# Graph attention on Trainium2: the clip of the exponentials moved from ScalarE and VectorE to GpSimd, the stage written without loops

## The reference

```python
q = (embeds[rows] @ qW).reshape(e, HEADS, dh)
k = (embeds[cols] @ kW).reshape(e, HEADS, dh)
v = (embeds[cols] @ vW).reshape(e, HEADS, dh)
scores = jnp.clip(jnp.einsum('ehd,ehd->eh', q, k), -10.0, 10.0)
exp_s = jnp.exp(scores)
norms = jax.ops.segment_sum(exp_s, rows, num_segments=nvar)[rows]
w = exp_s / (norms + 1e-08)
res = jax.ops.segment_sum(w[:, :, None] * v, rows, num_segments=nvar).reshape(nvar, d)
```

## Time and profile before

| | |
|---|---|
| median of 3 runs | 2467.38 us (2464.18 to 2469.9) |
| span of the profiled execution (its own time is given as this span) | 2467.5 us |
| VectorE busy in it | 1956.1 us |
| ScalarE busy in it | 1285.4 us |
| TensorE matmuls busy in it | 2131.4 us |
| GpSimd busy in it | 591.3 us |
| attention: first `masked` starts, last `sums_out` ends | 1007.83 us, 1489.84 us |

### The profile page before, as it was taken

One profiled execution on the slowest core, in us unless ns is written; L12 is line 12 of the kernel. 1 busy time (PEld: TensorE's weight loads), 2 busy tenths in 40 slices (PEclk: granted clock), 3 DMA queues, 4 the chain that ended last, 5 costly groups with the idle time before them and its releaser, 6 DMA issues. The chain is left out here.

```text
span 2467.5 us, 64202 instructions
## 1 busy us (share of the span) xinstructions
PE 2131.4 (86%) x22305; PEld 1792.1 (73%) x22306; DVE 1956.1 (79%) x2888; ACT 1285.4 (52%) x2996; POOL 591.3 (24%) x879
## 2 busy tenths in 40 slices
PE   2888887899999998776766666999999999999897
PEld 2777777899999998211111113799998599999787
DVE  8899998655565665899999996888887698888446
ACT  1888888333333332899999994432221622221323
POOL 3444443000000000200000001355554255555000
PEclk8999999899999999999999996999999999999799
DMA  2344444100010100511111113423233423232810
GB/s 67 147 165 170 167 168 160 69 29 28 28 41 29 41 15 14 140 47 41 42 42 41 42 41 129 138 73 85 73 86 64 181 72 86 72 86 45 299 43 21
DMA packets 94267, 205.36 MB, mean 83 GB/s; under 512 B 21204, under 2 KB 60756, under 8 KB 93952
## 3 DMA queue, kind: packets, MB, share of 16 engines
q1 hardware_dynamic: 80384, 182.39, 21.2%
q0 software_dynamic: 13696, 20.25, 4.3%
HBM read 116.99 MB, written 84.76 MB: 82 GB/s over the span
## 5 line engine op out<-in xcount | busy, mean ns | idle before, releaser
L1884 PE MATMUL l_bank<-tab,mask 128*128 128x192 f16 x7600 | 637.9, 247 | 7.3 <-PEq L1715 3.5
L1884 PEld LDWEIGHTS l_bank<-tab,mask 128*128 128x128 f16 x7600 | 630.9, 98 | 10.0 <-issue 9.3
L1470 DVE TENSOR_SCALAR mask<-code 128x1600 int32<-128x1600 int32 x304 | 543.7, 1815 | 95.8 <-PE l_bank L1884 70.6
L1860 POOL DMA_INDIRECT ggot<-table_dram,gidx x408 | 387.1, 949 | 265.4 <-PE l_bank L1884 204.9
L1351 DVE SCALAR_TENSOR_TENSOR pr<-ex,cring 128x1568 f32<-128x1568 f32 x200 | 356.3, 1782 | 0.0
L1289 PE MATMUL att_acc<-pr,v 128*32 128x392 f32 x1600 | 179.0, 520 | 147.6 <-DVE pr L1351 137.9
L891 PE MATMUL sums<-onehots,ct 128*128 128x192 f16 x3125 | 264.7, 248 | 11.3 <-issue 4.9
L891 PEld LDWEIGHTS sums<-onehots,ct 128*128 128x128 f16 x3125 | 261.8, 99 | 14.1 <-issue 7.6
L891 PE MATMUL sums<-u,ct 128*128 128x192 f16 x3125 | 259.1, 246 | 0.0
L891 PEld LDWEIGHTS sums<-u,ct 128*128 128x128 f16 x3125 | 258.0, 98 | 0.0
L1325 ACT ACTIVATE ex<-score_rest,poss 128x1176 f32<-128x1176 f32 x200 | 248.2, 1241 | 0.9 <-PE score_rest L1281 0.9
(11 more groups left out here) (349 smaller groups left out, 3143.0 us busy)
## 6 DMA issues: line engine op xcount, KB each, us to landing
code<-code_dram SPq DMA_DIRECT2D x38, 800.0 KB
code_dram<-flat SPq DMA_DIRECT2D x100, 200.0 KB, 1.9
ct_dram<-ct SPq DMA_DIRECT2D x25, 800.0 KB, 3.5
c_dram<-flat SPq DMA_DIRECT2D x25, 800.0 KB, 3.4
ct_again<-ct_dram SPq DMA_DIRECT2D x25, 800.0 KB, 16.9
cring<-c_dram SPq DMA_DIRECT2D x200, 98.0 KB, 1.9
table_dram<-tab SPq DMA_DIRECT2D x50, 384.0 KB, 2.3
flat<-code_dram SPq DMA_DIRECT2D x19, 800.0 KB, 4.4
```

Source lines behind the costliest of these rows:

```text
L1470: e.tensor_scalar(turned.rearrange("p (s q d) -> p s q d", q=NQ, d=DQ // 2), words.rearrange("p (q s d) -> p s q d", q=NQ, d=DQ // 2), abs ...
L1860: e.indirect_dma_start(ggot[:, k, j, :], None, table_dram[:, :], bass.IndirectOffsetOnAxis(ap=gidx[:, k, j:j + 1], axis=0)).then_inc(s_ggo ...
L1884: mm = e.matmul(acc[k][:, 0:2 * D], mask[:, r % MR, s, :], tab[:, s, r, :], start=(r == 0 and s == 0), stop=(r == R - 1 and s == NT - 1))
```

## The change

GpSimd clips the exponentials of all four heads on both sides with one `tensor_scalar` (min, max) of 128x1568 fp32, in place in `ex`, for each of the 200 tiles. VectorE is left with one `tensor_tensor` multiply of 128x1568 by the counts, which it reads from `cring` in SBUF as before. ScalarE has two plain Exps of 128x784, a pair of heads each, from two PSUM pairs. `acc` has two halves, so that the next block's sums start without waiting for the copy. AHEAD is 4. All eight blocks are written out without hardware loops. The relation weights are issued by SP at tile 27 and no longer by GpSimd; the maxima over them are taken at tile 75, and the `partition_all_reduce` stands behind GpSimd's last clip.

```diff
@@ gpsimd
+                        def clipped(n):
+                            e.wait_ge(s_ex[1], n + 1)
+                            ins = e.tensor_scalar(ex[n % UR][:], ex[n % UR][:], EXP_HIGH, EXP_LOW, ALU.min, ALU.max)
+                            ins.then_inc(s_clip, 1)
...
-                        load_relations(e, 0, s_bd_in)
+                        for n in range(TILES):
+                            clipped(n)
+                            if n == NT:
+                                e.wait_ge(s_pieces[2], 64)
+                                e.memset(bd[:], 0.0).then_inc(s_pad, 1)
+                                e.wait_ge(s_pad, 2)
                         e.wait_ge(s_bd, 2)
                         e.partition_all_reduce(btop[:], bmost[:], P, bass.bass_isa.ReduceOp.max).then_inc(s_bd, 1)
@@ sync
+                        for n in range(CR, TILES):
+                            if n in COPIES:
+                                load_copies(e, *COPIES[n])
+                            if n == RELATIONS_AT:
+                                e.wait_ge(s_pad, 2)
+                                load_relations(e, 0, s_bd_in)
+                            e.wait_ge(s_pr, n - CR + 1)
+                            load_counts(e, n)
@@ tensor
+                        for n in range(1, TILES):
+                            if n + AHEAD < TILES:
+                                scores(n + AHEAD, 0)
+                            sums(n)
+                            if n + AHEAD < TILES:
+                                scores(n + AHEAD, 1)
@@ scalar
-                            e.activation(short[j % UR][:], first_ps[:, 0:QC], ACT.Relu, bias=ten[:],
-                                         scale=negs[:]).then_inc(s_short, 1)
...
-                            e.activation(ex[j % UR][:, 1:H, :], rest_ps[j % 2][:, :, 0:QC], ACT.Exp,
-                                         scale=poss[:]).then_inc(s_rest, 1)
...
-                            e.activation(ex[j % UR][:, 0, :], short[j % UR][:], ACT.Exp, bias=ten[:],
-                                         scale=-1.0).then_inc(s_ex, 1)
...
+                        for n in range(TILES):
+                            for k in range(2):
+                                e.wait_ge(s_sc[k], n + 1)
+                                if k == 0 and n >= UR:
+                                    e.wait_ge(s_pr, n - UR + 1)
+                                e.activation(ex[n % UR][:, k * HP2:(k + 1) * HP2, :], pair_ps[k][:, :, 0:QC], ACT.Exp,
+                                             scale=poss[:]).then_inc(s_ex[k], 1)
@@ vector
-                            e.tensor_scalar(ex[j % UR][:, 1:H, :], ex[j % UR][:, 1:H, :], EXP_HIGH, None,
-                                            ALU.min).then_inc(s_capped, 1)
...
-                            e.scalar_tensor_tensor(pr[j % UR][:], ex[j % UR][:], EXP_LOW,
-                                                   cring[:, j % CR, :].unsqueeze(1).to_broadcast([P, H, QC]),
-                                                   ALU.max, ALU.mult).then_inc(s_pr, 1)
...
+                            e.wait_ge(s_c[n % CR], 16 * (n // CR + 1))
+                            e.wait_ge(s_clip, n + 1)
+                            if n >= UR:
+                                e.wait_ge(s_pv, n - UR + 1)
+                            e.tensor_tensor(pr[n % UR][:], ex[n % UR][:],
+                                            cring[:, n % CR, :].unsqueeze(1).to_broadcast([P, H, QC]),
+                                            ALU.mult).then_inc(s_pr, 1)
```

More of the change, by code:

```diff
@@ L1174, in _ @@
                         e.dma_start(vw[:], a["vW"]).then_inc(s_vw, 16)
-                        for j in range(CR):
-                            load_counts(e, 0, j)
+                        for n in range(CR):
+                            load_counts(e, n)
                         store_piece(e, 0)
@@ L1230, in gnn_kernel @@
                 UR = 5
-                short = [sb(f"short{k}", [P, QC], F32) for k in range(UR)]
                 ex = [sb(f"ex{k}", [P, H, QC], F32) for k in range(UR)]
                 pr = [sb(f"pr{k}", [P, H, QC], F32) for k in range(UR)]
-                ten = sb("ten", [P, 1], F32)
                 poss = sb("poss", [P, 1], F32)
[L1236 to L1241, removed]
+                HP2 = H // 2
+                pair_ps = [main.enter_context(nc.psum_tensor(f"score_pair{k}", [P, HP2, 512], F32)) for k in range(2)]
+                acc = main.enter_context(nc.psum_tensor("att_acc", [P, 2, 512], F32))
+                s_sc = [sem(f"l1_score{k}") for k in range(2)]
+                s_ex = [sem(f"l1_ex{k}") for k in range(2)]
+                s_cc, s_clip, s_pr, s_pv, s_acc, s_poss, s_pad = (
+                    sem("l1_" + k) for k in ("cc", "clip", "pr", "pv", "acc", "poss", "pad"))
                 s_bd, s_bd_in = sem("l1_bd"), sem("l1_bd_in")
-                AHEAD = 3
+                AHEAD, CAHEAD, OUT = 4, 3, 3
+                TILES = NQB * NT
+                RELATIONS_AT = NT + 2
+                LARGEST_AT = 3 * NT
                 with nc.Block() as block:
@@ L1270, in _, with scores @@
                     @block.tensor
                     def _(e):
-                        def scores(b, j, first=False):
-                            if first and j in first_keys:
+                        def scores(n, k):
+                            b, j = divmod(n, NT)
+                            if k == 0 and b == 0 and j in first_keys:
                                 e.wait_ge(s_spread[1][first_keys.index(j)], SPREAD)
[L1275 to L1287, removed]
+                            if k == 0 and n == NT:
+                                for piece in (1, 2):
+                                    e.wait_ge(s_spread[0][piece], SPREAD)
+                            if n:
+                                e.wait_ge(s_ex[k], n)
+                            for h in range(HP2):
+                                mm = e.matmul(pair_ps[k][:, h, 0:QC], ka[0:D, k * HP2 + h, j * P:(j + 1) * P],
+                                              qa[0:D, k * HP2 + h, b * QC:(b + 1) * QC], start=True, stop=True)
@@ L1288, in sums @@
+                            mm.then_inc(s_sc[k], 1)
+                        def sums(n):
+                            b, j = divmod(n, NT)
+                            e.wait_ge(s_pr, n + 1)
+                            if j == 0 and b >= 2:
+                                e.wait_ge(s_acc, b - 1)
                             for h in range(H):
-                                mm = e.matmul(acc[h * HW:(h + 1) * HW, 0:QC], v[:, j, h, :], pr[j % UR][:, h, :],
+                                mm = e.matmul(acc[h * HW:(h + 1) * HW, b % 2, 0:QC], v[:, j, h, :], pr[n % UR][:, h, :],
@@ L1293, in _ @@
                         first_keys = [b0 * QB // P for b0, _ in PIECES]
[L1294 to L1304, removed]
@@ L1306, in _ @@
-                        e.wait_ge(s_spread[0][0], SPREAD)
[L1307 to L1315, removed]
+                        FIRST = first_keys[1]
@@ new lines, in _ @@
+                        assert QC <= QB and 2 <= FIRST <= AHEAD
+                        e.wait_ge(s_spread[0][0], SPREAD)
+                        for n in range(FIRST):
+                            scores(n, 0)
+                            scores(n, 1)
+                        sums(0)
+                        for n in range(FIRST, AHEAD + 1):
+                            scores(n, 0)
+                            scores(n, 1)
+                        for n in range(1, TILES):
[4 more added lines that the diff above has]
+                                scores(n + AHEAD, 1)
@@ L1331, in _ @@
[L1331 to L1336, removed]
+                        e.wait_ge(s_poss, 1)
+                        for n in range(TILES):
[5 more added lines that the diff above has]
+                                             scale=poss[:]).then_inc(s_ex[k], 1)
@@ L1355, in sums_out @@
-                        def sums_out(b):
[L1357 to L1362, removed]
-                                    capped(b, j + 1)
-                                elif not last:
-                                    capped(b + 1, 0)
-                                masked(b, j)
-                                if first and j == NT - 1:
-                                    e.wait_ge(s_bd_in, 16 * LOADS)
-                                    e.tensor_reduce(bmost[0:D, 0:1], bd[0:D, :, 0:HW2], mybir.AxisListType.XY, ALU.max,
-                                                    apply_absolute_value=True).then_inc(s_bd, 1)
-                                    e.tensor_copy(bmost[:, 1:2], irregular[:]).then_inc(s_bd, 1)
-                                if j == 0 and not first:
-                                    sums_out(b - 1)
@@ L1385, in _, with masked @@
[L1385 removed]
+                        def masked(n):
+                            e.wait_ge(s_c[n % CR], 16 * (n // CR + 1))
```

(14 more changed lines are left out.)

31 lines of the change are left out of this document (3 added, 28 removed).

## The result

The changed kernel takes 2590.52 us (median of 4 runs, 2584.92 to 2592.64) against 2465.8 us before: 1.0501 times the time before, 95% interval 1.0485 to 1.0517, so 125 us slower. The forecast was 211 us slower, 2679 us. The sign and the mechanism were right, the size was not: the change costs 0.59 of what was forecast, and the time lies at the very lower edge of the range, 2590. (That bound was rounded down: 2612.5 less 0.1 us for each of 200 tiles is 2592.5, above what was measured.)

A forecast was written before the change was run, and what follows sets the result against it. VectorE was taken to bound attention at 2.38 us a tile; 1.70 multiply plus 1.72 clip made 3.42, +208 us over 200 tiles, plus 3 for weight loads, on 2467.5: 2679 us, range 2590 to 2930.

The forecast's parts named there:

- VectorE sets the kernel before; 2.38 us a tile: Attention before the change: VectorE, busy 419.44 of 419.50 us, sets the pitch at 2.38 to 2.39 us for 200 tiles.
- The multiply costs what `masked` did: VectorE's remaining multiply in attention was priced as `masked`: 1.78 us long and 1.70 us in pitch.
- Clip and multiply take turns, whoever came first: In attention, GpSimd's clip and VectorE's two-input multiply exclude each other, so their times add: pitch 3.42 us, +208 us.
- T = 1.72 us: GpSimd's two-sided clip of 128x1568 fp32 per attention tile, scaled from the 882 ns CAST of 806 elements: 1.72 us.
- The lower end of my bounds: GpSimd's clip in attention priced from below by a write-only iota, 0.89 ns an element: 1.39 us, pitch 3.09, total 2612.
- The page overruled: For GpSimd's clip, the skill page's 1.03 cycles per element, 1.35 us and a sum about 74 us lower, was set aside.
- The rival without turns: In attention, clip and multiply run side by side, ScalarE sets 1.86 us a tile: 2366 us, chance 0.10.
- The rival of a dear clip: In attention, turns with a clip of 2.0 to 3.0 us: 2734 to 2934 us, chance 0.24; above 3.0, 0.09.
- TensorE's clock may fall and costs nothing: In attention, TensorE at 1.2 instead of 2.4 GHz would need some 3.3 us a tile, under the pitch: costed at nothing.
- SP's 18 loads, one stall of 2 to 4 us: Weight loads issued ahead of tile 27's counts: 7.1 us of issue, 1.9 until counts land, +3 us in the sum.
- The reduction behind the last clip costs nothing: At attention's end, GpSimd's reduction takes 0.4 to 2.8 us beside VectorE's last multiply, the last sums and copy: nothing added.

The follow-up runs named there:

- half clip: The changed kernel with GpSimd clipping two of the four heads (128x784), the other two left unclipped: 2462.61 us (one run), 2.33 us a tile.

## Why the prediction was right and wrong

- **VectorE sets the kernel before; 2.38 us a tile**: right, 2.40 with the work at block ends (478.0 us for 199 pitches). The clip put on VectorE again gives 2.60, as its rows foretold.
- **The multiply costs what `masked` did**: right, 1787 ns where nothing disturbs it, against 1782.
- **Clip and multiply take turns, whoever came first**: right, in both directions, and no slower hand-over than their streams. What the trace before showed with operations of 6 and 25 elements holds for ones of 1568.
- **T = 1.72 us**: this step failed. The clip's term in the pitch is 1.30 us, 0.42 less, and 0.42 x 200 = 84 us is nearly the whole miss of 88 (2679 - 2590.5). With 1.30 the sum reads 2467.5 + 200 x 0.62 + 3 = 2594.5; the last 4 us are the tile before, which cost 2.40 us and not 2.38. Two errors lie in T. First the row, 0.23 us: I scaled the CAST's 882 ns by the elements, its fixed part with them; the clip, free, reads 1493 ns. Second, and nearly as large at 0.19: I took a free span for what one turn costs. GpSimd's own pitch would not have told it either, as the two free clips at the start of attention start 1.47 us apart. The half clip tells it: its shortest span is 829 ns against 1484 for the whole one, so 655 ns for 784 elements, 1.31 us of stream in a whole clip and some 0.17 fixed, and the 1.31 are what a turn was seen to cost. The lower end of my bounds, the iota's 0.89 ns an element, was the nearest: 1.39.
- **The page overruled.** I set aside the Trainium skill's figure (GPSIMD Engine Reference, Elementwise — side-by-side cycle accounting), 1.03 cycles per element or an estimated 1.35 us, because of the int32 TENSOR_SCALAR. The clip of fp32 read 1493 ns free and 1.30 us in the turns, so the estimate is near what a turn costs and 0.14 us short of the free span; by it the sum would have been 2605, 14 us over the measured time. The int32 row was the wrong witness; that its conversions make its price wasn't tried.
- **The rival without turns** (2366 us) is what the kernel does once the counts come from PSUM: 2364.7. That these agree to 2 us is luck: the rival had ScalarE at 1.86 us a tile, and the pitch is 1.77, with the start and the end of the stage longer. The rival of a dear clip (T over 2.0) is excluded.
- **TensorE's clock may fall and costs nothing**: it fell, to 0.83, and `sums` and `scores` still waited, for `pr` and for ScalarE.
- **SP's 18 loads, one stall of 2 to 4 us**: the trace of the changed kernel shows 7.2 us of issue and one wait of 2.5 us. The issue rows, then the row of waits:

```profile
1084.00 6.49 SPq L349 DMA_DIRECT2D spare<-in_weights  x16
...
1091.24 7.33 SPq L1131 DMA_DIRECT2D cring<-c_dram  x7
```

```profile
DVE pr L1345 <- DMA cring<-c_dram: 2.5, 1, 2.5
```

- **The reduction behind the last clip costs nothing**: nearly. It started 5.99 us behind GpSimd's last clip, with nothing that it waited for in the records, and so ended 0.8 us behind VectorE's last copy. A gap of 7.12 us of the same kind stands ahead of the first clip. The row of the reduction:

```profile
1611.51 0.37 POOL L1265 PARTITION_ALL_REDUCE btop<-bmost  x1 [5.99 <-issue]
```

  The Trainium skill (GPSIMD Engine Reference, Instruction dispatch) has about 6 us for a first call of freshly loaded code; the gap of 5.99 us agrees, the one of 7.12 is a microsecond longer, and both stand where the instruction order has its ISA rows without operands. The run with a memset in place of the clip has neither gap. The gap at the end is hidden but for the 0.8 us. Of the one at the start 3.5 us are not: the first tile's exponentials were done at 1004.37 and its clip began at 1007.86, and in the run with the memset the stage's first multiply comes 3.5 us sooner after GpSimd's first memset (5.4 us against 8.9). The prediction had put this at nothing in its sum, and said that it might be a few us.

The missing loops weren't undone by themselves; the run with the clip on VectorE met its price of 2.59 us to 0.01, so it leaves them no visible share in the pitch.

## What to carry to other kernels

Before work moves from VectorE to GpSimd, look at how many SBUF inputs the VectorE instruction beside it has: if two, and the GpSimd one reads SBUF, add the two streams and don't take the longer one. Taking one input from PSUM, by an identity matmul where TensorE has room, turned 125 us of loss into 101 us of gain. And when two engines both read as busy with spans far above their usual ones, divide the pitch by what each takes alone before calling either slow.

## What the runs showed of the hardware

- Turns of long streams cost less than their spans: 1787 + 1493 = 3280 ns of free spans took 3.00 us in turns. With the clip's stream of 1.31 us from the half clip, that fits an exclusion that covers the streaming and not the fixed part of either. The Trainium skill (SBUF — State Buffer, Who interferes with whom) has two SBUF inputs contend with GpSimd's reads, and says of VectorE's two-port modes that the shared pair is held for the whole instruction; here, with two inputs, the pitch is 0.28 us shorter than whole instructions would make it.
- GpSimd can be starved: one reduction of two columns took 0.38 us alone, 2.81 in the kernel before, 29.4 beside multiplies back to back, and 322 beside multiplies that alternate with VectorE's clips (the profile calls spans of such instructions rough). Had anything waited for it, that would have been the cost.
- A multiply with its broadcast input in PSUM, fp32, is as fast as with fp16 in SBUF: 1786 against 1787 ns.
- A GpSimd write of 128x1568 fp32 takes 1407 ns beside multiplies of two SBUF inputs, which stayed at 1787 ns.
